# A pre-norm attention and feed-forward block on one core: four buffers of probabilities, loads on ScalarE's queue, another front and new orders

## The reference

```
q = ln(x) @ wq            per head 192 columns, of which the first 128 are used
k, v = ln(x) @ wkv        per head 128 + 128 columns
scores = q k^T * 192 ** -0.5, causal
probs = softmax(scores)
x = x + concat(probs v) @ wo
h = relu(s0 * ln(x) @ K0) * 2
h = relu(s1 * ei(h) @ K1) * 2
x = x + s2 * ei(h) @ K2   ei multiplies the last fifth of the columns by -4
```

## Time and profile before

| | us |
|---|---|
| median of 3 runs | 1293.31 (1290.9 to 1293.65) |
| the profiled execution | 1298.54 |
| its span | 1296.8 |
| PE busy | 1130.2 (87%) |
| DVE busy | 887.9 (68%) |
| ACT busy | 682.7 (53%) |
| POOL busy | 680.6 (52%) |
| queue q1 (all DMAs), share of 16 engines | 55.5% |

### The profile page before, as it was taken

The page is one execution under the profiler, slowest core; times in us unless marked ns, Lnnn a source line. Parts: engine busy times, 40 slices in busy tenths (PEclk is TensorE's granted clock), DMA queues, the critical chain, the costliest instruction groups (busy, mean ns, idle before and its releaser), DMA issues. The chain is left out here.

```text
span 1296.8 us, 22420 instructions
## 1 busy us (share of the span) xinstructions
PE 1130.2 (87%) x6214; PEld 675.2 (52%) x6214; DVE 887.9 (68%) x1799; ACT 682.7 (53%) x1335; POOL 680.6 (52%) x694
## 2 busy tenths in 40 slices
PE   3576989889898979988898979988997989989898
PEld 1433555545555545544555545645554555556567
DVE  3655768576676767676677858766676767768783
ACT  3544546455555555555555645545555555555543
POOL 1234756455565755545575745555575546656310
PEclk8778999999999999998999999989999999999999
DMA  2155674756655684755556574746556485644501
GB/s 99 46 77 74 90 115 85 100 105 99 87 89 89 93 113 85 102 108 85 73 87 118 94 104 94 101 95 95 69 92 113 85 103 108 101 69 85 120 16 65
DMA packets 368376, 117.54 MB, mean 91 GB/s; under 512 B 313568, under 2 KB 362208, under 8 KB 368352
## 3 DMA queue, kind: packets, MB, share of 16 engines
q1 hardware_dynamic: 368352, 117.25, 55.5%
HBM read 39.59 MB, written 2.12 MB: 32 GB/s over the span
## 5 line engine op out<-in xcount | busy, mean ns | idle before, releaser
L1104 PE MATMUL psC<-xb,wqk 128*128 128x512 f16 x1350 | 333.8, 387 | 9.5 <-DVE xb L872 9.1
L1104 PE MATMUL psS<-qkT 128*128 128x512 f16 (+3 forms) x1152 | 239.1, 341 | 116.4 <-DVE p L976 112.1
L543 POOL TENSOR_TENSOR qkT<-qk,qkT 128x512 f16<-128x512 f32 x124 | 142.4, 1159 | 366.9 <-ACT qkT L708 366.9
L976 DVE SCALAR_TENSOR_TENSOR p<-psS,p 128x128 f16<-128x128 f32 (+7 forms) x256 | 193.2, 755 | 182.6 <-ACT p L725 177.1
L969 DVE CUSTOM_DVE_ANT_0 psS<-psS,mask,undo_qk 128x128 f32<-128x128 f32 (+7 forms) x256 | 210.3, 823 | 109.4 <-PE psS L1104 95.5
L715 ACT ACTIVATE psS<-psS,negmax 128x128 f32<-128x128 f32 (+7 forms) x256 | 183.1, 715 | 159.8 <-DVE negmax L969 157.7
L1104 PE MATMUL psC<-wos,attn 128*128 128x512 f32 x768 | 254.2, 452 | 9.4 <-DVE attn L959 4.8
L725 ACT ACTIVATE p<-psS 128x128 f16<-128x128 f32 (+7 forms) x256 | 166.1, 649 | 182.0 <-DMA pT<-p 165.0
L1104 PEld LDWEIGHTS psS<-qkT 128*128 128x128 f16 x1152 | 98.9, 100 | 227.4 <-DVE p L976 131.4
L1215 PE MATMUL psC<-pT,v 128*128 128x512 f16 (+3 forms) x1152 | 210.1, 338 | 2.2 <-issue 1.6
L1104 PEld LDWEIGHTS psC<-xb,wqk 128*128 128x128 f16 x1350 | 126.2, 99 | 164.6 <-issue 44.8
(11 more groups left out here) (88 smaller groups left out, 923.1 us busy)
## 6 DMA issues: line engine op xcount, KB each, us to landing
raw<-in_L_attn_wkv SPq DMA_DIRECT2D x64, 256.0 KB, 3.8
raw<-in_L_attn_wq SPq DMA_DIRECT2D x32, 256.0 KB
raw<-in_L_attn_wo SPq DMA_DIRECT2D x32, 256.0 KB
pT<-p SPq DMA_TRANSPOSE x256
wrow<-wmax_rows SPq DMA_DIRECT2D x48, 64.0 KB, 3.8
res<-in_L_attn_hidden_states SPq DMA_DIRECT2D x8, 256.0 KB, 6.2
out<-res SPq DMA_DIRECT2D x8, 256.0 KB, 2.0
wmax_rows<-wmax SPq DMA_DIRECT2D x48, 0.5 KB
```

Source lines behind the costliest of these rows:

```text
L543: nc.gpsimd.tensor_tensor(lo, qk32[:, AT[n], :], hi, ALU.subtract) \
L976: nc.vector.scalar_tensor_tensor(parts[:, :, LO, :], psS[:, n % 2, 0:(n + 1) * P].rearrange("p (k s) -> p k s", s=P), UP, parts[:, :, HI, ...
L1104: last = nc.tensor.matmul(out_ap, w, x, start=k == 0, stop=k == len(terms) - 1)
```

## The change

- p16 gets four buffers, and `turned` four semaphores: `h(n)` waits for the transpose of row n-4. x32, which shared p16's memory, moves to pT.
- The loads, `put` and `get` are no longer in SP's list but in ScalarE's (`loading_step(act, ...)`); head 0's, head 1's first ones and those of the front stay with SP. SP's list holds transposes alone.
- In the front the first two bounds (head 0's, and the values' of the first pair) take the row of sums from two TensorE transposes of a broadcast column (`spread`), not through DRAM; VectorE does the first bound ahead of the norm's statistics, ScalarE does both high halves of head 0's weights ahead of the norm's root, and SP issues all loads of the front without a wait.
- The waits for loaded q and k are one semaphore for each parity of the head; a wait of GpSimd for xn is gone.
- All orders and the string BANKS are new.

In the diff, `...` marks what is left out. The bodies of `load_head`, `load_out`, `load_values`, `rows_to_dram` and `rows_from_dram` are those of before, with the queue as an argument.

```diff
@@ -38,36 +38,38 @@
 
 
 TENSOR_ORDERS = ("""
-    pv1@-1 s2@0 v0@0 s3@0 v1@0 x1@1 s4@0 o4@-1 s5@0 v2@0 x2@1 v3@0 s6@0 x3@1 s7@0 x4@1 o5@-1 x5@1 o6@-1 x6@1 o7@-1
-    x7@1 v4@0 pv0@0 v5@0 s0@1 v6@0 o0@0 s1@1 v7@0 o1@0 s2@1 o2@0 s3@1 o3@0 pv1@0 s4@1 s5@1 x1@2 o4@0 x2@2 o5@0 s6@1
-    o6@0 x3@2 s7@1 x4@2 o7@0 x5@2 pv0@1 x6@2 x7@2 o0@1 o1@1 o2@1 o3@1 s0@2 s1@2""", """
-    y0@2 y1@2 turn4@2 turn5@2 turn6@2 turn7@2 v0@2 v1@2 v2@2 v3@2 y2@2 s0@2 y3@2 s1@2 v4@2 s2@2 v5@2 s3@2 v6@2 x1@3
-    s4@2 v7@2 x2@3 s5@2""", "")
+    pv1@-1 s4@0 v0@0 x1@1 s5@0 o4@-1 x2@1 v1@0 s6@0 o5@-1 v2@0 x3@1 v3@0 x4@1 s7@0 x5@1 x6@1 v4@0 x7@1 o6@-1 v5@0
+    pv0@0 s0@1 o7@-1 v6@0 s1@1 v7@0 o0@0 s2@1 o1@0 s3@1 o2@0 pv1@0 s4@1 o3@0 s5@1 x1@2 o4@0 x2@2 s6@1 x3@2 o5@0 x4@2
+    s7@1 x5@2 o6@0 x6@2 o7@0 x7@2 pv0@1 s0@2 o0@1 s1@2 o1@1 o2@1 s2@2 o3@1 s3@2""", """
+    y0@2 y1@2 turn4@2 turn5@2 turn6@2 turn7@2 v0@2 v1@2 v2@2 s0@2 v3@2 y2@2 s1@2 y3@2 s2@2 v4@2 s3@2 v5@2 s4@2 v6@2
+    s5@2 v7@2 x1@3 s6@2 x2@3""", "")
 
 SCALAR_ORDERS = ("""
-    e7@-1 h7@-1 pv0@-1 qk3@0 qk2@0 r0@1 e0@0 h0@0 e1@0 qk1@0 h1@0 mx0@2 pv1@-1 e2@0 v0@0 h2@0 e3@0 h3@0 v1@0 snap0@1
-    e4@0 h4@0 v2@0 e5@0 h5@0 v3@0 e6@0 h6@0 e7@0 qk0@1 mx1@2 qk3@1 h7@0 qk2@1 v4@0 pv0@0 qk1@1 v5@0 e0@1 h0@1 r0@2
-    v6@0 e1@1 h1@1 v7@0 mx0@3 e2@1 h2@1 e3@1 h3@1 pv1@0 e4@1 h4@1 snap0@2 e5@1 h5@1 r1@2 qk0@2 e6@1 h6@1""", """
-    khi0@2 nhi0@2 nhi1@2 nhi2@2 nhi3@2 mx1@2 keep0@2 keep1@2 keep2@2 keep3@2 r1@2 vhi0@2 vhi1@2 y0@2 root1@2 y1@2
-    mx0@3 nhi4@2 nhi5@2 nhi6@2 nhi7@2 keep4@2 keep5@2 keep6@2 keep7@2 v0@2 v1@2 v2@2 v3@2 r0@3 y2@2 y3@2 e0@2
-    part0@2 h0@2 v4@2 e1@2 part1@2 h1@2 v5@2 e2@2 h2@2 part2@2 v6@2 snap0@3 part3@2 e3@2 h3@2 v7@2""", "")
+    e4@-1 h4@-1 snap0@0 e5@-1 h5@-1 mx0@1 e6@-1 r1@0 qk0@0 put0@1 lo0@-1 h6@-1 e7@-1 h7@-1 qk2@0 pv0@-1 lo0@0 get0@1
+    lqk0@2 qk1@0 e0@0 h0@0 e1@0 h1@0 qk3@0 r0@1 e2@0 h2@0 pv1@-1 e3@0 h3@0 v0@0 mx0@2 e4@0 h4@0 e5@0 snap0@1 h5@0
+    v1@0 e6@0 put0@2 v2@0 qk0@1 h6@0 v3@0 get0@2 lv0@2 e7@0 lqk0@3 h7@0 qk3@1 r0@2 v4@0 qk2@1 mx1@2 v5@0 put1@2 e0@1
+    h0@1 pv0@0 get1@2 v6@0 qk1@1 e1@1 h1@1 v7@0 e2@1 h2@1 e3@1 h3@1 pv1@0""", """
+    nhi0@2 nhi1@2 mx1@2 nhi2@2 nhi3@2 keep0@2 keep1@2 keep2@2 keep3@2 r1@2 root1@2 y0@2 vhi0@2 vhi1@2 y1@2 nhi4@2
+    nhi5@2 nhi6@2 nhi7@2 mx0@3 keep4@2 keep5@2 keep6@2 keep7@2 v0@2 v1@2 v2@2 e0@2 h0@2 v3@2 r0@3 y2@2 e1@2 h1@2
+    y3@2 e2@2 h2@2 part0@2 v4@2 e3@2 h3@2 part1@2 v5@2 e4@2 h4@2 v6@2 e5@2 h5@2 part2@2 v7@2 part3@2 snap0@3 e6@2
+    h6@2""", "")
 
 VECTOR_ORDERS = ("""
-    a7@0 o0@-1 sc0@1 m0@0 m1@0 l0@0 o1@-1 l1@0 o2@-1 o3@-1 m2@0 pv1@-1 rv0@0 m3@0 l2@0 v0@0 l3@0 v1@0 m4@0 o4@-1
-    m5@0 l4@0 a2@1 v2@0 l5@0 m6@0 a3@1 v3@0 m7@0 a4@1 o5@-1 l6@0 a5@1 o6@-1 a6@1 a7@1 o7@-1 l7@0 v4@0 pv0@0 m0@1
-    sc0@2 l0@1 v5@0 m1@1 o0@0 v6@0 l1@1 m2@1 v7@0 o1@0 m3@1 l2@1 o2@0 sc1@2 o3@0 l3@1 m4@1 pv1@0 m5@1 l4@1 o4@0 a2@2
-    o5@0 l5@1 m6@1 o6@0 a3@2 m7@1 l6@1 o7@0 a4@2 l7@1 a5@2 pv0@1 a6@2""", """
-    nlo0@2 nlo1@2 nlo2@2 nlo3@2 stat4@2 stat5@2 sc1@2 stat6@2 stat7@2 scale1@2 y0@2 apply4@2 apply5@2 apply6@2
-    apply7@2 y1@2 nlo4@2 nlo5@2 nlo6@2 nlo7@2 v0@2 v1@2 v2@2 sum0@2 v3@2 sc0@3 sum1@2 y2@2 sum2@2 m0@2 y3@2 sum3@2
-    m1@2 v4@2 l0@2 part0@2 l1@2 m2@2 part1@2 v5@2 m3@2 l2@2 part2@2 v6@2 l3@2 part3@2 m4@2 v7@2""", "")
+    m1@0 l0@0 o0@-1 l1@0 sc0@1 m2@0 m3@0 o1@-1 l2@0 o2@-1 o3@-1 pv1@-1 l3@0 v0@0 m4@0 m5@0 o4@-1 l4@0 a2@1 m6@0 v1@0
+    l5@0 v2@0 o5@-1 a3@1 l6@0 rv0@0 a4@1 m7@0 v3@0 a5@1 sc0@2 a6@1 l7@0 a7@1 v4@0 v5@0 o6@-1 m0@1 o7@-1 l0@1 pv0@0
+    m1@1 v6@0 l1@1 m2@1 v7@0 o0@0 l2@1 m3@1 sc1@2 o1@0 l3@1 o2@0 m4@1 o3@0 pv1@0 m5@1 l4@1 o4@0 a2@2 m6@1 l5@1 a3@2
+    o5@0 a4@2 m7@1 l6@1 a5@2 o6@0 a6@2 a7@2 l7@1 pv0@1 o7@0 m0@2""", """
+    nlo0@2 nlo1@2 nlo2@2 nlo3@2 sc1@2 stat4@2 stat5@2 stat6@2 stat7@2 scale1@2 apply4@2 apply5@2 apply6@2 apply7@2
+    y0@2 y1@2 nlo4@2 nlo5@2 nlo6@2 nlo7@2 v0@2 v1@2 sum0@2 m0@2 v2@2 l0@2 v3@2 sum1@2 sc0@3 y2@2 m1@2 l1@2 sum2@2
+    y3@2 m2@2 l2@2 sum3@2 v4@2 m3@2 l3@2 part0@2 v5@2 m4@2 l4@2 part1@2 v6@2 m5@2 l5@2 part2@2 v7@2 m6@2 l6@2
+    part3@2""", "")
 
 SYNC_ORDERS = ("""
-    t1@-1 put0@1 t2@-1 t3@-1 get0@1 t4@-1 t5@-1 lqk0@2 t6@-1 t7@-1 t0@0 t1@0 t2@0 put0@2 t3@0 lo0@0 lqk0@3 t4@0
-    get0@2 lv0@2 t5@0 t6@0 put1@2 lo0@1 t7@0 get1@2 t0@1""", """
+    t0@0 t1@0 t2@0 t3@0 t4@0 t5@0 t6@0 t7@0 t0@1 t1@1 t2@1 t3@1 t4@1 t5@1 t6@1 t7@1""", """
     lqk0@3 put0@3 get0@3 lo0@2""", "")
 
 POOL_ORDERS = ("""
-    sum0@1 wv2@0 qk0@1 wo0@0 qk2@1 qk3@1 qk1@1 wqk0@2 sum0@2 qk0@2 wv0@2 wo0@1 wv1@2 qk2@2 qk3@2 wqk0@3 qk1@2""", """
+    wv0@0 qk0@0 wo0@-1 qk2@0 qk1@0 wv1@0 qk3@0 wqk0@1 sum0@1 qk0@1 wv2@0 qk3@1 wqk0@2 qk2@1 wo0@0 qk1@1 sum0@2""", """
     wqk0@2 wk0@2 wv0@2 wv1@2 wqk0@3 sum0@3""", "")
 
...
@@ -75,7 +77,7 @@
 CHAINS = ("x", "y", "v", "pv", "o")
 NB = 4
 
-BANKS = "301201230123012301230123012012301230123012"
+BANKS = "301230120123012301230123012301230123012012"
 FFN_CHAINS = ([(0, n) for n in range(4)] + [(1, n) for n in range(4)] + [(0, n) for n in range(4, 8)]
               + [(2, 0), (2, 1)] + [(1, n) for n in range(4, 8)] + [(2, n) for n in range(2, 8)])
...
@@ -94,6 +96,8 @@
 
     h = GH * g + step[1]
     if h == 0 and (step[0] in ("x", "a", "snap", "sum", "qk", "mx", "sc", "r", "put", "get", "lqk", "lv") or step[0] == "wv" and step[2] == 2):
+        return False
+    if h == 1 and (step[0] == "lqk" or step[0] in ("put", "get") and step[2] == 0) or h == 0 and step[0] == "lo":
         return False
     return 0 <= h < HEADS
...
@@ -226,7 +230,7 @@
 
         res = sb("res", [P, NT, D], F32)
         v = sb("v", [P, 2, NT, GH * DN], F16)
-        p16 = sb("p16", [P, 2, 2 * S], F16)
+        p16 = sb("p16", [P, 4, 2 * S], F16)
         qkT = sb("qkT", [P, 5, 2, CH], F16)
         attn = sb("attn", [P, 2, CH], F32R)
...
@@ -266,7 +270,7 @@
         h1T = [sb(f"h1T{k}", [P, 2, DC, CH], F32R) for k in range(NC)]
 
         x32 = [t.rearrange("p a s -> p (a s)").bitcast(F32).rearrange("p (k c s) -> p k c s", k=2, c=2)
-               for t in (p16[:, :, :], pT[:, 1, 0:32, :])]
+               for t in (pT[:, 1, 32:64, :], pT[:, 1, 0:32, :])]
         t32 = [t[:, :, :].rearrange("p (k c) s -> p k c s", c=2) for t in (xn, qk32)]
         X11, X21, X12, X22 = (x32[k // 2][:, k % 2] for k in range(4))
...
@@ -359,7 +365,7 @@
 
         def parts_of(n):
 
-            return p16[:, n % 2, 0:2 * (n + 1) * P].rearrange("p (k w s) -> p k w s", w=2, s=P)
+            return p16[:, n % 4, 0:2 * (n + 1) * P].rearrange("p (k w s) -> p k w s", w=2, s=P)
 
         def qk_slot(j, n):
...
+
+            at = 2 if n else j % 2
+            if n:
+                wait_pair(q, rows_max[1], g, 1, j, 1)
+                q.sem_inc(queue_go, 1)
+                wait_pair(q, rows_in[1], g, 16, j, -16)
+            else:
+                wait(q, rows_max[0], g, 1, j, 1)
+                q.sem_inc(queue_go, 1)
+                wait(q, rows_in[0], g, 16, j, -32)
+            q.dma_start(wmax_dram[at:at + 1, :].rearrange("a p -> p a"), wmax[:, at:at + 1]) \
+                .then_inc(rows_out[n], 16)
+
+        def rows_from_dram(q, g, j, n):
+
+            at = 2 if n else j % 2
+            if n:
+                wait_pair(q, rows_out[1], g, 16, j, 0)
+                q.sem_inc(queue_go, 1)
+                wait_pair(q, bounded[1], g, 4, j, -3)
+            else:
+                wait(q, rows_out[0], g, 16, j, 0)
+                q.sem_inc(queue_go, 1)
+                wait(q, bounded[0], g, 5, j, -9)
+            q.dma_start(wrow[:, at, :], wmax_dram[at, :].partition_broadcast(P)).then_inc(rows_in[n], 16)
+
+
+        def loading_step(q, g, step, j, n):
+
+            if step == "lqk":
...
         @block.sync
         def _(sp):
-            load_head(0, 0)
+            load_head(sp, 0, 0)
             for t in range(4):
                 sp.dma_start(res[:, t, :], x_v[:, t, :]).then_inc(x_in[t], 16)
-            rows_to_dram(-1, 2, 0)
-            rows_from_dram(-1, 2, 0)
-            load_values(0)
+            load_values(sp, 0)
             for t in range(4, NT):
                 sp.dma_start(res[:, t, :], x_v[:, t, :]).then_inc(x_in[t], 16)
-            rows_to_dram(-1, 2, 1)
-            rows_from_dram(-1, 2, 1)
             for n, s in enumerate((s0, s1, s2)):
                 sp.dma_start(scl[:, n:n + 1], s.partition_broadcast(P)).then_inc(scl_in, 16)
 
...
-                        sp.dma_start_transpose(pT[:, j % 2, rows_of(n), :], p16[:, n % 2, 0:2 * (n + 1) * P]) \
-                            .then_inc(turned[n % 2], 16)
+                        sp.dma_start_transpose(pT[:, j % 2, rows_of(n), :], p16[:, n % 4, 0:2 * (n + 1) * P]) \
+                            .then_inc(turned[n % 4], 16)
+                    else:
+                        loading_step(sp, g, step, j, n)
...
@@ -687,12 +691,12 @@
                 at = 2 if n else j % 2
                 if n:
                     wait_pair(act, loaded["v"], g, 32, j, 32)
-                    wait_pair(act, rows_out[1], g, 16, j, 0)
```

(43 more changed lines are left out.)

90 lines of the change are left out of this document (33 added, 57 removed).

## The result

The changed kernel takes **1434.18 us** (1431.59 to 1436.34) where the kernel before takes 1293.48: a ratio of 1.109 with the interval [1.106, 1.112]. The forecast was 1357, in a range of 1225 to 1400. The direction was right, the forecast change of +64 us was less than half of the +141 that came, and the time lies outside the range.

A forecast was written before the change was run, and what follows sets the result against it. TensorE's order was taken to set the time, so only its gaps could change. The front's -13 us and +77 us from 14.5 turns at +5.3 gave +64 on 1293.3, so 1357 us, range 1225 to 1400.

The forecast's parts named there:

- the idle time of a turn: TensorE's gaps in one loop turn: waits removed, three stalls and new gaps added, +5.3 us in sum (-6.4+6.9 to +9.8).
- third stall: Load of wo (lo0@-1) behind put0@1 on ScalarE's queue lands late, delaying o0@-1 and s2@0: 2.7 us a turn (1.5 to 4).
- the front: Before the loop: first bounds by TensorE transposes instead of DRAM make the start earlier, -13 us (-8 to -19).
- First stall: At get0@2: ScalarE waits for the put, the row reaches VectorE's sc0@2 late, pv0@0 is 3.0 us late (1.8 to 4.2).
- Second: Stall at get1@2: ScalarE waits for put1@2 ahead of e1 and h1, s3@1 is 4.6 us late (3.6 to 5.3).
- The orders' own gaps: Gaps on TensorE from the new orders themselves, 0 to 2.7 us a turn, taken as 1.4.
- The removed wait: ScalarE's 10.7 us a turn of waiting for transposes goes with four buffers, giving TensorE all 6.4 us a turn.
- The put's length: A put of row bounds to DRAM needs about 7.3 us from its issue, alone.
- Rival A: A put on its own queue lands in about 3 us, so no stall exists: about 1201 us, chance 0.12.
- Rival C: Puts beside another queue's transposes take 10 us or more, two stalls grow by 2.5 us each: about 1430, chance 0.08.

The follow-up runs named there:

- a1_spread: Changed kernel with put and get for the rows replaced by TensorE transposes into psS, loads still on ScalarE's queue: 1190.2 us, ratio 0.920.
- a2_lo_early: Changed kernel with the load lo0@-1 (wo) issued at the head of ScalarE's turn, ahead of put0@1 instead of behind it: 1375.3 us, ratio 1.064.
- c1_oldloop: Kernel before with the new front and four buffers; its loop orders, bank string and one queue stay: 1236.2 us, ratio 0.957.
- b1_four: Kernel before with four buffers of probabilities instead of two and nothing else: 1232.2 us, ratio 0.955.
- c5_one_queue: Changed kernel with all loads and small transfers back on SyncE's queue, in a list written for the new orders: 1339.7 us, ratio 1.036.
- c3_old_spread: c1_oldloop with the rows spread by TensorE transposes instead of through DRAM, and three buffers for the squares: 1133.1 us, ratio 0.876.

## Why the prediction was wrong

The span grew by 133 us where the sum had +64, 69 too little. Three terms of the sum make these 69, by the means of thirteen turns above and 14.5 turns: TensorE's clock, which the sum left out, 2.4 x 14.5 = 35; the idle time of a turn, +6.7 where +5.3 was forecast, 1.4 x 14.5 = 20, and it is the third stall that was too small; and the front, whose -13 did not come, 14.

**The missing term**: TensorE's clock. The sum had only idle time, and no sentence of the prediction says why the work itself should take as long as before. The mean turn has 12.3 us at a granted clock of 0.50, where it had 5.5, and 2.4 us more of busy time; in all TensorE was busy 35.2 us longer. In a1_spread, without the gaps, the clock is 1.00 and the same work takes 64.8 us a turn. The kernel before already showed a share of this: its clock was 0.98 in the earlier trace rows, and 0.96 over the thirteen turns.

**Third stall**: the wait that was off most; forecast 2.7 with an upper end of 4, measured 5.4 on the mean and 5.8 in the turn shown. Two things in it were mis-sized. I let the load behind the put land 7.6 us after it, though the earlier trace rows has 9.6 us for such a load; it was 11.8 to the split, and 10.7 to landing in the timed transfers, behind the kernel's end. And I took o0@-1 and ScalarE's lo0@0 for the ones who wait, while on GpSimd qk2@0 stands behind the split of wo, and s0@0 needs that, with the next scores in its train. The rule that I had given for ScalarE (what is queued behind the waiting instruction?) I didn't apply to GpSimd. a2_lo_early gave back 4.1 us a turn for this stall alone.

**The front**: the marks came as forecast (18.45 for the first product, 23.81 for the second transposes, 41.78 for head 1's sum, against near 18, 25.5 and 43.7). But the -13 us was taken from a mark in the middle and never followed to the loop: 14.5 turns at +9.1 make 132 of the span's 133 us, so nothing of it is left. c1_oldloop against b1_four shows it given back at the waits of 7.65 and 4.43 us above, and the changed kernel has such waits too, 6.75 us at 47.00 and 4.43 at 67.87. Of 13 us, 4.5 were left at the end of the two profiled spans (1226.4 against 1230.9), none that the medians show.

**First stall**: forecast 3.0, measured 3.0 on the mean (3.6 in the turn shown), by the mechanism named (the row reaches VectorE's sc0@2 late); c5_one_queue shows that it doesn't need ScalarE's waiting. **Second**: forecast 4.6, measured 4.3; in c5_one_queue, where ScalarE doesn't stand, it is all but gone. **The orders' own gaps**: forecast 1.4, measured 0.7 in the turn shown.

**The removed wait** was right: none of the 10.7 us is left. The 6.4 us were read in a turn of 72.5 us, shorter than the mean one. b1_four gained 61 us where 6.4 x 14.5 = 93 was the most: b1_four and c1_oldloop show TensorE waiting some 3.4 us a turn for pT<-p (51.0 us in 15 waits of b1_four), which the kernel before doesn't have, so part of the gain turned into that.

**The put's length** was right for a put alone, 7.2 to 7.6 us; in the loop it was longer, 8.5 in the median and 11.6 at most. Rival A fell with it.

Put together, for a mean turn: -7.2 for all of TensorE's idle time before, +3.0 + 4.3 + 5.4 for the stalls and +1.2 for the rest is +6.7, and 2.4 more for the clock, where there was 0: +9.1.

**Rival C** named 1430, which is nearly the measured time, but that is luck for the most part: it had stalls one and two grow by 2.5 us each over the forecast's 3.0 and 4.6, and they came at 3.0 and 4.3. Its true part is that a put with a load right behind takes longer than 7.3 us, at the third stall.

What stays open: what each stall's half clock costs in time, since no run changed the clock without changing the gaps; what makes the 57 us between a1_spread and c3_old_spread; and why 4-byte pieces next to each other in DRAM are slow.

## What to carry to other kernels

Before moving waits to another engine's queue, write down for every engine, the one that only splits operands too, what stands behind the step that will be late, and give the stalls of the bounding engine a second term for the half clock behind them, which here was 35 us of busy time beside 98 us of idle time. Ask first why a wait is long: the same 128 numbers took 7.2, 2.0 or 1.4 us by where they were written, and the edit of that transfer was worth as much (181 us) as all moves of steps together (180).

## What the runs showed that was not expected

- 128 pieces of 4 bytes from a column: 7.2 us into one contiguous row of DRAM, 1.4 us with 64 or 512 bytes between them, 2.0 us into a row of SBUF; the row in one piece to DRAM 1.1 us.
- A transpose issued 0.4 us behind a put of the other queue took 7.1 us instead of 4.2, and landed with it. A load of wo issued 0.4 us behind a put of its own queue landed after 10.3 us.
- The mean wo product (128x512, f32) took 487 ns in the changed kernel and 438 in c3_old_spread. The same shape from the same tiles, at a mean granted clock of 0.93 and 0.99; that the clock is all of it isn't shown (the page of each, the kernel after first):

```profile
L1113 PE MATMUL psC<-wos,attn 128*128 128x512 f32 x768 | 283.0, 487 | 6.1 <-DVE attn L968 6.0
```

```profile
L1113 PE MATMUL psC<-wos,attn 128*128 128x512 f32 x768 | 244.9, 438 | 4.8 <-DVE attn L968 4.7
```
